# A gated cross-attention and mixture-of-experts block: context, Wq, Wk and biases laid out by the host, SyncE's order rewritten, expert weights in two buffer pairs, list entries spread over the tiles, small tiles four deep

## The reference

```
q = layernorm(x) @ Wq + bq ; k = ctx @ Wk + bk ; v = ctx @ Wv + bv     (16 heads of 16)
x = x + tanh(g0) * (softmax(q k^T / 4) v @ Wo + bo)
xt = layernorm(x) as 4096 tokens ; logits = xt @ Wr + br                (8 experts)
gate = softmax over the two largest logits of a token
y = sum over those two of gate * (relu(xt @ W1[e] + b1[e]) @ W2[e] + b2[e])   (256 -> 1024 -> 256)
x = x + tanh(g1) * y
```

## Time and profile before

| | |
|---|---|
| median of three runs | 882.1 us (879.96 to 883.54) |
| profiled execution, its own time | 884.82 us |
| its span | 883.1 us |
| mean granted clock of PE | 0.944 of full speed |
| PE / DVE / ACT / POOL busy | 753.8 / 612.7 / 407.7 / 438.3 us |
| DMA moved | 85.15 MB, 96 GB/s on average |

### The profile page before, as it was taken

One profiled execution on the slowest core, in us unless ns is written; L12 is line 12 of the kernel. 1 busy time (PEld: TensorE's weight loads), 2 busy tenths in 40 slices (PEclk: granted clock), 3 DMA queues, 4 the chain that ended last, 5 costly groups with the idle time before them and its releaser, 6 DMA issues.

```text
span 883.1 us, 22095 instructions
## 1 busy us (share of the span) xinstructions
PE 753.8 (85%) x6602; PEld 503.6 (57%) x6603; DVE 612.7 (69%) x1279; ACT 407.7 (46%) x784; POOL 438.3 (50%) x439
## 2 busy tenths in 40 slices
PE   3489988888888989875799789999999999999765
PEld 2145555545555555432567567767777777776543
DVE  5567899999797989974457767666666666666333
ACT  2046767776676767755233223333333333333220
POOL 5112433555555565436654745555555555554322
PEclk9579999999999999987799999999999999999788
DMA  4334655666565656544312233222222232223111
GB/s 131 109 106 120 190 167 177 185 180 171 161 168 159 182 169 179 150 111 131 91 25 38 31 45 46 47 48 48 48 48 48 48 48 48 48 42 49 26 20 23
DMA packets 96292, 85.15 MB, mean 96 GB/s; under 512 B 21702, under 2 KB 85516, under 8 KB 96108
## 3 DMA queue, kind: packets, MB, share of 16 engines
q1 hardware_dynamic: 80268, 65.72, 26.6%
q0 software_dynamic: 15680, 18.69, 13.6%
q10 hardware_dynamic: 288, 0.00, 0.0%
HBM read 53.61 MB, written 30.62 MB: 95 GB/s over the span
## 4 chain that ended last, share of the span: by engine, by line
PE 29%; DMA 26%; DVE 18%; issue 16%; POOL 5%; ACT 3%; SPq 1%; DVEq 1%; POOLq 1%; ACTq 0%
DMA out_dram<-yb,dest_idx 20%; DVE negmax L1081 6%; PE banks L1756 5%; PE banks L1658 4%; PE banks L1577 3%; DMA xg<-xn_rows,gather_idx 3%; PE banks L1554 3%; PE banks L1742 2%; PE banks L1744 2%; PE banks L1743 2%; ACT probs L882 2%; PE banks L1646 2%; DVE stats L1005 2%; POOL xg L688 2%; PE banks L1625 2%
## 5 line engine op out<-in xcount | busy, mean ns | idle before, releaser
L954 ACT ACTIVATE hid<-banks,b_col 128x256 f32<-128x256 f32 (+1 forms) x312 | 124.1, 451 | 238.7 <-PE banks L1744 128.1
L1756 PE MATMUL banks<-wall,hh 128*128 x568 | 210.1, 389 | 4.3 <-DVE yb L1495 4.1
L745 POOL DMA_INDIRECT out_dram<-yb,dest_idx x71 | 123.7, 1743 | 169.0 <-DMA out_dram<-yb,dest_idx 81.2
L1742 PE MATMUL banks<-xh,wall 128*128 128x256 f16 (+1 forms) x624 | 167.9, 272 | 15.7 <-DVE xl L1432 14.4
L1081 DVE TENSOR_REDUCE negmax<-banks 128x4 f32<-128x1024 f32 x128 | 155.8, 1217 | 27.8 <-PE banks L1625 27.2
L1743 PE MATMUL banks<-xl,wall 128*128 128x256 f16 (+1 forms) x624 | 167.8, 272 | 0.0
L1744 PE MATMUL banks<-xh,wall 128*128 128x256 f16 (+1 forms) x624 | 167.7, 272 | 0.0
L882 ACT ACTIVATE probs<-banks 128x1024 f32<-128x1024 f32 x128 | 131.1, 1024 | 67.8 <-PE banks L1646 67.3
L1756 PE MATMUL banks<-wall,hl 128*128 x568 | 147.4, 279 | 0.0
L1658 PE MATMUL banks<-probs,vaug 128*32 128x256 f32 x1024 | 84.0, 400 | 28.0 <-ACT probs L882 17.5
L688 POOL DMA_INDIRECT xg<-xn_rows,gather_idx x71 | 86.9, 1224 | 37.7 <-issue 21.2
(11 more groups left out here) (206 smaller groups left out, 1201.7 us busy)
## 6 DMA issues: line engine op xcount, KB each, us to landing
wst<-in_L_ffn_W SPq DMA_DIRECT2D x30, 512.0 KB, 5.1
k_parts<-kparts SPq DMA_DIRECT2D x48, 128.0 KB, 3.4
ks<-k_parts SPq DMA_DIRECT2D x64, 96.0 KB, 2.2
q_parts<-qparts SPq DMA_DIRECT2D x48, 128.0 KB, 2.0
qs<-q_parts SPq DMA_DIRECT2D x64, 96.0 KB
xin<-in_x SPq DMA_DIRECT2D x16, 256.0 KB, 5.4
cin<-in_ctx SPq DMA_DIRECT2D x16, 256.0 KB, 6.9
xres<-in_x SPq DMA_DIRECT2D x16, 256.0 KB, 4.8
```

What stands on the lines that cost most here:

```text
L745: nc.gpsimd.indirect_dma_start(out_rows, bass.IndirectOffsetOnAxis(dest_idx[par][:, s:s + 1], 0), yb[par][:, s, :], None, compute_op=ALU.a ...
L954: ins = nc.scalar.activation(hid[half][:, c % (HC // 2), 0:subs(j) * P], banks[:, b, c % 2 * TS:c % 2 * TS + subs(j) * P], ACT.Relu, bias= ...
L1742: nc.tensor.matmul(dst, hi, xh[par][:, m, 0:rows], start=(m == 0), stop=False)
L1756: ins = nc.tensor.matmul(dst, h_[:, c, s * P:(s + 1) * P], w_, start=(c == 0 and k == 0), stop=(c == HC - 1 and k == 1))
```

## The change

- **Layouts.** The host hands over ctx transposed (feature by token), Wq and Wk with the columns in the order that VectorE used to make, biases as columns. PE's context transposes go (16 times four), so do its bias transposes, VectorE's reordering and bias copies. ScalarE makes the context's high part from SBUF; the low part is made by VectorE for batches 0 and 1 and by **GpSimd** for 2 to 15, behind norm2 and one list entry, ahead of the last one.
- **Head.** K starts from the context alone, in bank 5, ahead of norm_T(0); K of batch 1 stands ahead of the first scores_max. SyncE stores K and Q parts, then loads them.
- **SyncE's body.** Weights come early, into `raw` or `wst` by turns; x and context of batch m+3 are loaded in body m; the second halves of K and Q parts of m+1 are loaded at the end of body m; xres is loaded a body earlier; results of x1b and xn2b are taken apart.
- **Late weights, tables, first gathers.** ScalarE takes six late weights in body 15 and two in 16 (before: four and four), VectorE five and three (before: three and five), the early tile table at slot 3 of body 15 instead of 6, gathers of tiles 0 and 1 at the end of body 15 instead of in 16.
- **Crossing.** turn_out(15) comes first, router(14) without the ranks, the last four slices of first(0) behind output(15). Ranks of pairs 6 and 7 are made in steps 0 and 2.
- **List entries.** Two in each of GpSimd's steps 1 to 4 (pair 6) and 6 to 9 (pair 7), each behind the gather of its step. TILE_LEAD goes from 8 to 14, bodies 12 and 13 are unrolled.
- **Small tiles.** Gathered four steps ahead into halves of `xg`; output in banks 6 and 7 by turns, so that second(j) waits for the result of j-2; VectorE takes the result of j-1 between the two halves of cut_hidden(j+1).

```diff
-        LEAD, PEELED, TILE_LEAD = 4, 6, 8
+        LEAD, PEELED, TILE_LEAD, TABLES_AT = 4, 6, 14, 7
...
+        def half_of(j):
+            return (j - BIGS) // 2 % 2
+        def y_bank(j, par, s):
+            return 6 + (s if subs(j) == SUB else par)
...
+        arrival = [raw, wst]
...
                 if attention:
                     max_row(m - 1, 1 - par, 1)
-                if post:
-                    residual(m - 2)
+                if weights:
+                    for w in range(2):
+                        e = t - 1
+                        wait(sp, stage_free[w], 2 * (t - 1) + par)
...
+                        sp.dma_start(stage_view(arrival[par][w], w), src).then_inc(w_full[par][w], 16)
...
                 if ahead:
                     load_part(m + 1, 1 - par, "q", 0)
...
+                if within(m, 0, NB - 4):
+                    load_x(m + 3, t, 1 - par)
...
+                if post:
+                    result_rows(m - 2)
+                if within(m, 1, NB):
+                    residual(m - 1)
+                if ahead:
+                    load_part(m + 1, 1 - par, "k", 1)
+                    load_part(m + 1, 1 - par, "q", 1)
...
+                if post:
+                    norm_rows(m - 2)
...
+            def gather_small(j, par):
+                h, turn = half_of(j), (j - BIGS) // 4
+                if turn == 0:
+                    hold(pool, xg_full[par], 16 * SUB * (BIGS // 2))
+                    hold(pool, gT_done, BIGS - 1 + par)
+                else:
+                    hold(pool, xg_half[par][h], 16 * turn)
+                    hold(pool, gT_done, j - 3)
...
+            def context_low(n, par):
+                hold(pool, ctxT_evac, n + 1)
+                nc.gpsimd.tensor_tensor(ctxT[par][:, 1].rearrange("p m t -> p (m t)"), cin[par][:].rearrange("p m t -> p (m t)"),
+                                        ctxT[par][:, 0].rearrange("p m t -> p (m t)"), ALU.subtract).then_inc(ctxT_split, 1)
...
+                if sending and par == 0:
                     paced(4, 5)
+                if turns:
+                    context_low(m + 2, par)
+                if sending and par == 0:
                     paced(5, 7)
...
+                elif j >= BIGS - 2:
+                    ahead = (2 * j - BIGS + 4, 2 * j - BIGS + 5) if j < BIGS else (j + 4,)
+                    for x_ in ahead:
+                        if x_ < NT:
+                            gather_small(x_, x_ % 2)
+                if fixed and 1 <= j < 5:
+                    send_entry(NB // 2 - 2, 2 * (j - 1))
+                    send_entry(NB // 2 - 2, 2 * (j - 1) + 1)
...
+                if fixed and 6 <= j < 10:
+                    send_entry(NB // 2 - 1, 2 * (j - 6))
+                    send_entry(NB // 2 - 1, 2 * (j - 6) + 1)
...
-                    wait(pe, y_ready, slot_at(j - 1) + s + 1)
+                    if subs(j) == SUB:
+                        wait(pe, y_ready, slot_at(j - 1) + s + 1)
+                    else:
+                        pe.wait_ge(y_ready, slot_at(j - 2) + 1 if j - 2 >= BIGS else slot_at(BIGS - 1) + 1 + par)
```

More of the change, by code:

```diff
@@ L500, in _ @@
                 store_part(0, 0, name)
-                for h in range(2):
+            for h in range(2):
+                for name in "kq":
                     load_part(0, 0, name, h)
@@ L700, in paced @@
                 def paced(n, v):
-                    hold(pool, exp_done, 8 * (m - 1) + v + 1)
+                    done = min(v, 2) if isinstance(m, int) and m == NB else v
+                    hold(pool, exp_done, 8 * (m - 1) + done + 1)
                     send_entry(t - 3, n)
@@ L978, in _ @@
             relu(0, e, 0)
-            relu(0, e, 1)
             attended_T(NB - 1)
-            relu(0, e, 2)
-            relu(0, e, 3)
+            for b in range(1, 4):
+                relu(0, e, b)
             high_x(1, 1)
@@ L1424, in _ @@
                 assert chain[0] == was + PER_LAP, (chain, was)
-            chain[0], chain[1] = was + (NB // 2 - 1 - PEELED // 2) * PER_LAP, 0
-            for m in range(NB - 2, NB + 1):
+            chain[0], chain[1] = was + (NB // 2 - 2 - PEELED // 2) * PER_LAP, 0
+            for m in range(NB - 4, NB + 1):
                 body(m // 2, m % 2)
@@ L1523, in step @@
                 if fixed and j == 5:
+                    entries(NB // 2 - 1)
+                if fixed and j == 6:
                     small_table()
-                if there(j, 1):
-                    for half in range(2):
+                for half in range(2):
+                    if there(j, 1):
                         cut_hidden(j + 1, 1 - i, half)
+                    if half == 0 and after_small and there(j, -1):
+                        result(j - 1, (j - 1) // 2, 1 - i, 0, e)
                 if fixed and j == 0:
                     router(NB - 1, 1, 7)
-                    listed_top(q)
+                    entries(NB // 2 - 2)
+                    carry_on(NB // 2 - 2)
+                    listed_top(NB // 2 - 1)
+                elif fixed and j == TABLES_AT:
+                    dve.wait_ge(table_ready, 6)
                 elif fixed and j == TILE_LEAD - 2:
@@ L1664, in turn_out @@
                     pe.wait_ge(av_evac, 4 * (n + 1))
-                    wait(pe, lg_evac, n)
+                    wait(pe, lg_evac, NB - 2 if isinstance(n, int) and n == NB - 1 else n)
                 else:
@@ L1786, in body @@
                             turn_max(m - 1, 1)
-                        if ahead:
+                        if ahead and not first_batch:
                             k(m + 1, 1 - par, 0)
```

429 lines of the change are left out of this document (193 added, 236 removed).

## The result

The changed kernel takes 852.1 us (median of 4 runs, 849.97 to 854.66) against 882.8 for the kernel before (879.96 to 884.21): ratio 0.9625, 95% interval 0.9583 to 0.9666. That is 31 us off, half of the 62 forecast; 822 and the range from 798 to 846 were too low. Measured times rest on all runs of a kernel, rows and stage times on its one profiled execution. The profiled execution took 851.28 us, its span is 849.5.

The account below looks back on a forecast made before the run. VectorE was taken as nearest to the bound in attention with PE just behind, latencies in head and small tiles, PE in later big tiles. Gains 8 + 11 + 9 + 6 + 28 = 62 us gave a forecast of 822, range 798 to 846.

Parts of the forecast that it names:

- Head: Start to K(2): earlier Q projection and store 5 us, K(1) moved into the wait 3; sum 8, bounds 4 and 12.
- Bodies: Twelve attention bodies: a VectorE subtraction and four PE transposes removed, 0.9 us each, 11 us; bounds 3 to 20.
- nearly all of 0.68 comes off: Attention bodies: VectorE, 90% busy with PE waiting for it, loses a subtraction of 678 ns, nearly all of it gained.
- rival (1): Attention: port contention and the late GpSimd subtraction eat the gain, stage gives 0 instead of 11: 833 us; chance 0.15.
- Rival (4): Attention: K(m+2) waits for GpSimd's subtraction, each us of delay costing one per body; 904 us at 5 us; chance 0.03.
- Last body and crossing: Last body to first tiles: earlier gather, router, tile 1's wait and clock, less two splits; sum 9, bounds 3 and 15.
- four hidden slices behind output(15) and fewer small VectorE operations ahead cover some 2: Crossing: of PE's 5.4 us wait for the low part of tile 1, some 2 us are covered.
- the 3 us for the gather before tile 0: Last body: GpSimd issues tile 0's gather in body 15, saving 3 of the 4.10 us that ScalarE waits for scores.
- First big tiles: Tiles up to 600 us: PE's gather waits fall from 10.0 us to 4; gain 6, bounds 0 and 9.
- 9.4 us a tile in the unrolled queue, 12.0 with entries: First big tiles: GpSimd's queue time per tile against PE's 10.7, slipping 1.2 us a step over eight steps.
- Small tiles: Last tiles: gathers four steps ahead and alternating output banks give 5.6 us steps, 36.7 against 64.7; gain 28, bounds 20 and 31.
- Rival (2): Small tiles find another loop, such as relu waiting for cuts, or half clock; steps 8 us, not 5.6: 837; chance 0.13.

Follow-up runs that it names:

- experiment 5: Changed kernel with the context's low part made by VectorE from SBUF in slot 7 again, instead of by GpSimd: 857.05 us, 0.9672 to the kernel before.
- Experiment 1: Changed kernel with GpSimd's addition of the residual's bias held until VectorE has made the low part of the attended rows: 850.92 us, 0.9609 to the kernel before.
- five_edits: Changed kernel with residual addition held, entries behind scatter, expert reads in big tiles, tile 1 turned early, small-tile result ahead of both cuts: 819.73 us, 0.9252.
- experiment 7: Changed kernel with tile 1's gathered rows turned ahead of tile 0's last four slices, its high and low parts ahead of relu's and cut's second half: 849.46 us.
- experiment 8: Two versions of the changed kernel: small tiles as before, 873.9 us; early tile table and gathers of tiles 0 and 1 as before, 854.83 us.
- experiment 10: five_edits with two of VectorE's late weight splits moved from body 15 to body 16: 824.61 us, 0.9245 to the kernel before.
- experiment 2: Changed kernel with a step's two list entries placed between its two scatters instead of ahead of both: 836.69 us, 0.9443 to the kernel before.
- experiment 4: Changed kernel with PE reading the expert numbers of all small tiles during the last two big tiles and keeping the registers: 850.93 us, 0.9586.
- experiments 3 and 4: Changed kernel with PE reading each expert number once instead of twice from the first small tile on, 850.62 us; all read during the last two big tiles, 850.93.

## Why the prediction was wrong

The stages of the two traces differ by 33.6 us in sum, of which 62 were forecast; the head brought more, the other four less. Three stayed below their own lower bounds: the crossing (3), the first big tiles (0) and the small tiles (20). The prediction named 852 for all terms at their lower bounds, but ended its range at 846, which its two lower bounds don't give either (838 at most).

**Head (8, measured 10.0).** Right. The first scores are at 25.00, where 25 to 26 stood, 5.5 us sooner; K(1) in the wait and the rest up to K(2) gave 4.5, where 3 stood.

**Bodies (11, measured 8.1).** The mechanisms were right, but two sizes were off. The first is "nearly all of 0.68 comes off" for VectorE: the move is worth 0.2 to 0.3 (experiment 5). So, with the collision gone, some 0.6 to 0.7 of a body's 0.9 come from the transposes and the new order of loads, to which the sum gave 0.2; no run separates these two. That the sum of a stage freed of its collision (10.8) meets the forecast (11) is luck in its parts. The contention was known from the earlier trace rows, but looked for at the new subtraction (1.15 to 1.85 us, mean 1.39; forecast 1.4). It came at the addition that I had just freed of its wait: I asked what the early xres would release, not what it would stand beside. And an overlap was priced at 0.6 against a mean that held overlaps itself; the addition alone takes 1.27 us, so that the earlier trace rows shows 0.8. Experiment 1's edit takes the collision away, and in five_edits the twelve bodies give 10.8. That is rival (1) with another instruction in it. Rival (4) didn't occur.

**Last body and crossing (9, measured 0.0).** The failed step has three parts. From K(15) on the change gained 3.1 us (108.7 before, 105.6 after), and body 13 took them back: it costs 25.06 us (332.36 - 307.30) instead of the 21.93 of before, by the collision above and the half clock after it. The nine traces with the collision have 23.2 to 25.3 there, the four without it 21.5 to 22.0. That "four hidden slices behind output(15) and fewer small VectorE operations ahead cover some 2" of the wait for tile 1 was right in size (5.4 to 3.2), but the remainder and its half clock are worth 4.3 (experiment 7). And the 3 us for the gather before tile 0 were read from ScalarE's 4.10 of idle time; PE's own wait for that gather was 1.17 us (at 411.04 of the trace before), and with the gathers late again the stage was as long as with them early (experiment 8). What of that is the table that moved with them stays open, as do the 2 us for two more splits in body 15 (experiment 10). With 1 and 7 the stage gives 9.9.

**First big tiles (6, measured -1.6).** The step that failed is "9.4 us a tile in the unrolled queue, 12.0 with entries". Each piece is a little longer in the queue than alone (scatter issue to 2.45, entries to 1.54, the wait for landing to 3.57), and a step with entries is 12.6 to 14.0. The slip of 1.7 to 3.1 us against PE's 10.9, in eight steps, is what the old bunches cost too. The sum was low by its own figures as well: eight steps of 1.2 us, less 1.7 at the start and 1.3 in step 5, leave 6.6 of waits and not 4. And I priced a PE wait at its length: with the clock that falls behind them, 10 us of waits were worth some 16 (experiment 2).

**Small tiles (28, measured 17.1).** "5.6" for a step left out the two register reads. The five steps took 34.5 us instead of 28.0, 6.5 more; four of them are 6.8 to 7.2 with the reads and 5.3 to 5.5 without (experiment 4), some 6 us, while the first, from tile 31 on, is 6.7 and 6.6. Rival (2) was right that there is another bound; relu and the cuts, its example, weren't it. Then, I stopped at the last tile's first instruction, where 6.4 us were left before. Now 13.5 are left, 7.1 more: 3.3 up to the last scatter, as the scatters queue, 4.58 and 4.65 us apart (841.20 - 835.96 = 5.2, before 878.64 - 876.72 = 1.9), and 3.9 behind it, in the DRAIN whose cause is open. Against that, the last two steps took 5.9 us to this point and not 8.7, 2.8 less: the 3.5 that I had put down for the queue (whose working is not given; two scatters at 4.7 in place of 2.6 would be 4.2) mostly came later. 6.5 + 7.1 - 2.8 = 10.8 is what was missing, to a tenth.

## What to carry over

When a wait is taken from GpSimd or VectorE, whose instructions hold each other up, look up what the next instruction will then stand beside, on the other engine and ahead of which wait: a four-column instruction there can cost 1.7 us. Put issues that nobody waits for into an existing wait of their queue, not ahead of it; here two entries cost 2.6 us a step in one place and nothing three lines further down. Price a stall of the matrix engine with the half clock behind it, read a wait's size from the engine that bounds the stage, and count the sum to the end of the program, not to the last compute. Ahead of reading a stage's gain from two traces, look how much that stage varies in traces that share it.

## What the runs showed that was not expected

- The share (4 columns) took 1.87 us from 314.37, and ended with GpSimd's addition at 316.20, though that began only at 314.92. The list entry alone doesn't hold it: in experiment 1 the share stands as far into the same entry and takes 0.16 us. So it takes the addition queued behind the entry, and what holds VectorE in the 0.55 us before the addition starts is open. The Trainium skill (SBUF — State Buffer, Who interferes with whom) has the pair of ports held for a whole instruction; by that rule, the trace agrees from 314.92 on.
- A read of a number from SBUF into a PE register costs 0.6 to 0.8 us among matmuls of 128 columns and next to nothing among those of 256 (experiments 3 and 4).
- Waits of 0.2 to 0.9 us, the same in two kernels, were followed by 10 us at 1.2 GHz in one and at 2.4 GHz in the other (experiment 10). K(15) to the first result differed by 5.6 us; how much of that is this one drop isn't shown. Single traces of this kernel's stages differ by 5 us with no cause in the code (tile 0 to tile 31: 357.6 to 363.0).
- The end of GpSimd's program, from the start of the last scatter, lasts 8.2 to 8.3 us in all kernels with the change and 4.4 in the one before. Nothing in the rows tells why.
